# Two Strassen passes instead of two plain ones and one Strassen pass, in the second of two gated MLP blocks

## The reference, cut to what matters

```python
# block 1
n = ln(x)
s = silu(n @ w_gate.T)                     # 1376 a token
s = where(|s| is among the 688 smallest of its row, 0, s)
x = x + ln((s * (n @ w_up.T)) @ w_down.T)
# block 2
n = ln(x)
x = x + ln((silu(n @ W_gate.T) * (n @ W_up.T)) @ W_down.T)
```

## Time and profile before

| | |
|---|---|
| median of three runs | 733.29 us |
| profiled execution | 734.79 us, span 733.0 us |
| granted TensorE clock, mean | 0.998 of full speed |
| TensorE busy | 719.5 us (98%) |
| VectorE busy | 533.0 us (73%) |
| ScalarE busy | 370.0 us (50%) |
| GpSimd busy | 183.8 us (25%) |
| block 1, up to the end of down(15) | to 397.8 us of the span, chunks of block 2 among it |
| Strassen pass, products | 556.7 to 666.6 us |
| its down projections | 666.6 to 727.1 us |

### The profile page before, as it was taken

How to read it: one execution, slowest core, us unless ns; L and a number is a source line. 1 busy time by engine, 2 the same in 40 slices (tenths; PEclk the granted TensorE clock), 3 DMA queues, 4 the chain that set the end, 5 groups by cost and what they waited for, 6 DMA issues and landing times.

```text
span 733.0 us, 9630 instructions
## 1 busy us (share of the span) xinstructions
PE 719.5 (98%) x3235; PEld 603.9 (82%) x3235; DVE 533.0 (73%) x954; ACT 370.0 (50%) x592; POOL 183.8 (25%) x322
## 2 busy tenths in 40 slices
PE   8999999999999999999999999999999999999996
PEld 7888788888888888888888887888878787777885
DVE  6789688888877788897887544555557888887442
ACT  5886577767666666667645331222234333233321
POOL 0422232333322233323301000200026444520010
PEclk9999999999999999999999999999999999999999
DMA  8641435433445535565834422353414333234431
GB/s 275 195 111 60 94 107 127 119 82 118 107 129 135 124 81 140 135 160 143 295 121 117 125 42 57 58 130 72 87 32 141 116 114 108 81 125 140 146 127 43
DMA packets 109123, 86.50 MB, mean 118 GB/s; under 512 B 65520, under 2 KB 89072, under 8 KB 108880
## 3 DMA queue, kind: packets, MB, share of 16 engines
q1 hardware_dynamic: 109072, 85.88, 42.5%
HBM read 53.08 MB, written 22.09 MB: 103 GB/s over the span
## 4 chain that ended last, share of the span: by engine, by line
PE 73%; issue 8%; DVE 8%; POOL 5%; ACT 4%; DMA 1%; POOLq 0%; SPq 0%; DVEq 0%
PE gu_ps L748 16%; PE y_ps L727 12%; PE gu_ps L713 11%; PE tr_ps L713 8%; PE tr_ps L769 5%; PE gu_ps L802 5%; PE gu_ps L816 4%; PE tr_ps L802 4%; PE tr_ps L816 3%; ACT junk L940 2%; POOL move L1809 2%; PE y_ps L769 2%; POOL thr L1812 1%; PE y_ps L802 1%; DVE below L1388 1%
## 5 line engine op out<-in xcount | busy, mean ns | idle before, releaser
L940 ACT ACTIVATE junk<-absv,thr 128x1383 bf16<-128x1383 f32 x96 | 139.2, 1450 | 49.6 <-POOL thr L1812 48.9
L727 PE MATMUL y_ps<-down_hi,hT 128*128 128x512 f32 x352 | 108.9, 390 | 0.0
L727 PEld LDWEIGHTS y_ps<-down_hi,hT 128*128 128x128 f32 x352 | 66.1, 188 | 14.5
L727 PE MATMUL y_ps<-down_lo,hT 128*128 128x512 f32 x176 | 69.4, 394 | 0.8 <-DVE hT L1306 0.8
L713 PE MATMUL gu_ps<-gate_hi,xT 128*128 128x460 f32 (+1 forms) x232 | 67.2, 371 | 0.0
L713 PE MATMUL gu_ps<-up_hi,xT 128*128 128x460 f32 (+1 forms) x232 | 67.2, 371 | 0.0
L1809 POOL TENSOR_SCALAR move<-sgn 128x1 f32<-128x1 f32 x80 | 40.6, 507 | 93.2 <-ACT junk L940 93.1
L1793 POOL TENSOR_TENSOR yrstd<-yvar,half 128x1 f32<-128x1 f32 x32 | 18.7, 583 | 132.1 <-DVE yvar L1315 131.8
L1786 POOL TENSOR_TENSOR xrstd<-xvar,half 128x1 f32<-128x1 f32 x32 | 18.7, 584 | 130.2 <-DVE xvar L1278 130.2
L713 PEld LDWEIGHTS gu_ps<-up_hi,xT 128*128 128x128 f32 x232 | 43.6, 188 | 5.1
L713 PEld LDWEIGHTS gu_ps<-gate_hi,xT 128*128 128x128 f32 x232 | 43.7, 189 | 4.9
(11 more groups left out here) (329 smaller groups left out, 1813.2 us busy)
## 6 DMA issues: line engine op xcount, KB each, us to landing
absv<-prod SPq DMA_DIRECT2D x64, 176.0 KB, 3.4
xin<-x_scratch SPq DMA_DIRECT2D x20, 256.0 KB, 2.8
h_scratch<-prod SPq DMA_DIRECT2D x20, 256.0 KB, 2.5
xres<-in_L_attn_x SPq DMA_DIRECT2D x16, 256.0 KB, 5.2
x_scratch<-xres SPq DMA_DIRECT2D x16, 256.0 KB, 3.2
xin<-in_L_attn_x SPq DMA_DIRECT2D x13, 256.0 KB, 3.6
xT<-xin SPq DMA_DIRECT2D x52, 64.0 KB, 2.4
xg_even<-xin SPq DMA_DIRECT2D x48, 64.0 KB, 2.5
```

The lines of the kernel that those rows point to most:

```text
L727: last = nc.tensor.matmul(y_ps[:, :], h, w[:, c, :], start=(c == 0 and i == 0), stop=(c == JC - 1 and i == 2))
L940: nc.scalar.activation(junk[:, 0:I + PAD], absv[:, q, A0 - PAD:A0 + I], ACT.Sign, bias=thr[:, q:q + 1], scale=-1.0, accum_out=sgn[:, q:q + ...
```

## The change

The two plain groups go. Block 2 has two Strassen passes, tiles 0 to 7 and 8 to 15, 22 units in all. With it change:
- Seven products go to seven fixed banks, in the order 1, 2, 3, 6, 5, 7, 4 (`PSEQ`); product i of a unit waits until product i of the unit before has been read (`product_read`).
- The four weight sums of a chunk are the same in both passes. GpSimd makes them in block 1, in tiles 4 to 10 (`left_sum`, `SUMS_AT`), two chunks a tile and then one; SP stores them in `left_scratch`, and `load_left` loads all seven factors, in three DMAs.
- Left factors have four places a, b, c, d (`PLACES`) instead of three. `left_lo(u + 1)` stands ahead of `gate0(u)`, from unit 4 on.
- The copies of the weights in DRAM are gone. `load_down` loads the down weights once, and `split_pair_lo` for them goes from VectorE to GpSimd, in units 5 to 10 of pass 1. `right_sum` and `h1` go to GpSimd too.
- Tiles 16 to 23 (the tokens of pass 1) are normalised in block 1, two x tiles a tile in tiles 7 to 14 (`TWO`) instead of 11 to 14. Of pass 2, four x tiles are normalised in units 5 to 8 of pass 1 (`X_AT`) and four in the down tiles between the passes (`XD`).
- Units 0 to 3 of pass 1 are mixed with the end of tiles 14 and 15 of block 1.

```diff
-    PLAIN = S0 // GT
-    PSEQ7 = [1, 2, 6, 5, 3, 7, 4]
-    M_AT = {(u, i): 7 * u + n + 1 for u in range(JC) for n, i in enumerate(PSEQ7)}
+    PASSES = 2
+    S_TILES = 2 * GT
+    UNITS = PASSES * JC
+    PSEQ = [1, 2, 3, 6, 5, 7, 4]
+    M_AT = {(u, i): 7 * u + n + 1 for u in range(UNITS) for n, i in enumerate(PSEQ)}
+    PLACES = "bdcbdcabdab" + "abcabcabcab"
...
+        SUMS_AT = {4: (0, 1), 5: (2, 3), 6: (4, 5), 7: (6, 7), 8: (8,), 9: (9,), 10: (10,)}
+        PAIR_AT = {5: (0,), 6: (1,), 7: (2,), 8: (3,), 9: (4,), 10: (5,)}
+        R_AT = {2: (1,), 3: (2,), 5: (3,), 6: (6, 5), 7: (7, 4)}
+        LEFT_AT = {3: JC, 4: JC + 1}
+        X_AT = {5: 24, 6: 25, 7: 26, 8: 27}
+        XD = {0: (28,), 1: (29,), 2: (30,), 3: (31,)}
...
@@ tensor
             down(TILES - 3)
-            for m in range(2):
-                chunk(0, 0, m)
-                chunk(0, 1, m)
+            strassen(0, PSEQ[:4])
             down(TILES - 2)
-            for j in range(2, 4):
-                chunk(0, j, 0)
-                chunk(0, j, 1)
+            strassen(0, PSEQ[4:])
+            strassen(1)
+            strassen(2)
+            strassen(3)
             down(TILES - 1)
...
+            for u in range(4, JC):
+                strassen(u)
+            for r in range(S_TILES):
+                down_tile(r)
+            for u in range(JC, UNITS):
+                strassen(u)
+            for r in range(S_TILES, 2 * S_TILES):
+                down_tile(r)
...
@@ vector: hand-over from block 1, then pass 1
+            swap_h(last - 1)
+            right_lo(0, 1)
+            left_lo(0)
+            right_lo(0, 2)
+            y_stats(last - 2)
+            right_lo(0, 3)
+            right_lo(0, 6)
+            split_h_lo(last - 1)
+            add_residual(last - 2)
+            for n in range(3):
+                times_up(last, n)
...
+            for u in range(3, JC):
+                if FULL <= u < JC - 1:
+                    left_lo(u + 1)
+                gate0(u)
+                sum_u2(u)
+                if u == 4:
+                    y_stats(last)
+                sum_u4(u)
+                gate1(u)
+                if u == 3:
+                    left_lo(u + 1)
+                elif u == 4:
+                    add_residual(last)
+                elif u in X_AT:
+                    x_stats(X_AT[u])
+                    x_normalise(X_AT[u])
+                if u == JC - 1:
+                    tile_lo(0, 0)
+                sum_u3(u)
+                up1(u)
+                up0(u)
+                h0(u)
...
@@ gpsimd
-            def left_sums(u):
-                pool.wait_ge(l_in[u % 3], 32 * (u // 3 + 1))
-                a21, a22, a11, a12, s1, s2, s3, s4 = (left_raw(u, LEFT.index(i)) for i in (0, 4, 1, 2, 5, 6, 7, 3))
...
+            def split_pair_lo(k):
+                j, n = PAIRS[k]
+                pool.wait_ge(phi_done, k + 1)
+                size = P if j + n < JC else LASTJ
+                at = slice(0, size), slice(j, j + n), slice(0, H)
+                nc.gpsimd.tensor_tensor(down_lo[at], down_lo_raw[at], down_hi[at].bitcast(F32),
+                                        ALU.subtract).then_inc(plo_done, 1)
+
+            def h1(u):
+                pool.wait_ge(silu1_done, u + 1)
+                pool.wait_ge(up1_done, u + 1)
+                at = s_part("sum1", u)[0:width(u), :]
+                nc.gpsimd.tensor_tensor(at, at, s_part("gate1", u)[0:width(u), :], ALU.mult).then_inc(h1_done, 1)
...
+                for n in range(STEPS):
+                    if n == 3:
+                        if j in TWO and XSEQ[p + 2] < TILES + S_TILES:
+                            x_rstd(XSEQ[p + 2])
+                        y_rstd(j - 2)
+                    newton(j, n)
+                    for u in SUMS_AT.get(j, ())[1:] if n < 4 else ():
+                        left_sum(u, n)
             last = TILES - 1
+            right_sum(0, 5)
             units(last)
-            for n in range(3):
-                newton(last, n)
+            newton(last, 0)
+            right_sum(0, 6)
+            newton(last, 1)
+            right_sum(0, 4)
+            newton(last, 2)
+            right_sum(0, 7)
             newton(last, 3)
             y_rstd(last - 2)
             newton(last, 4)
+            h1(0)
+            for u in range(1, JC):
+                if u == 4:
+                    y_rstd(last)
+                elif u in X_AT:
+                    x_rstd(X_AT[u])
+                h1(u)
+                if u == 1:
+                    y_rstd(last - 1)
+                for k in PAIR_AT.get(u, ()):
+                    split_pair_lo(k)
```

More of the change, by code:

```diff
@@ L120, in moved, with width, earlier, sum_place @@
         return POS[a] - FIRST
-    def width(j):
-        return P if j < JC - 1 else LASTJ
+    def width(u):
+        return P if u % JC < JC - 1 else LASTJ
+    def earlier(u):
+        return PLACES.rindex(PLACES[u], 0, u) if PLACES[u] in PLACES[:u] else None
+    def sum_place(u):
+        if u < 3:
+            return (0, 2, 0)[u]
+        return u % JC % 2
+    def stores_before(u):
+        return sum(sum_place(v) == sum_place(u) and v % JC < JC - 1 for v in range(u))
     ctx = ExitStack()
@@ L1660, in _ @@
+            right_lo(0, 4)
+            left_lo(1)
+            gate0(0)
+            sum_u2(0)
             find_below(last)
-            split_h_lo(last - 1)
-            add_residual(last - 2)
-            split_pair_lo(NPAIR + 1)
+            sum_u4(0)
+            gate1(0)
             find_top(last)
+            sum_u3(0)
+            up1(0)
+            up0(0)
+            h0(0)
+            left_lo(2)
             find_flag(last)
+            gate0(1)
+            sum_u2(1)
             select(last)
+            sum_u4(1)
@@ L1667, in _ @@
+            gate1(1)
             swap_h(last)
-            times_up2(0)
-            split_h2_lo(0)
-            times_up2(1)
-            split_h2_lo(1)
+            sum_u3(1)
+            up1(1)
+            up0(1)
+            h0(1)
+            left_lo(3)
             y_stats(last - 1)
-            for k in (2, NPAIR + 2):
-                split_pair_lo(k)
+            gate0(2)
+            sum_u2(2)
+            sum_u4(2)
+            gate1(2)
             add_residual(last - 1)
+            sum_u3(2)
@@ L1736, in _ @@
+            for u in range(JC, UNITS):
+                if JC < u < UNITS - 1:
+                    left_lo(u + 1)
                 gate0(u)
```

1013 lines of the change are left out of this document (432 added, 581 removed).

## The result

The changed kernel takes 753.79 us (median of four runs, 753.49 to 753.83), the kernel before 733.60 (732.73 to 734.17): a ratio of 1.028, interval 1.026 to 1.029. I had forecast 738 with a range up to 747. The sign was right, the size was not. In what follows "the port" is, as in the prediction, the access to SBUF on which GpSimd's operations and those of VectorE that have two operands in SBUF exclude each other; "the first block" is block 1.

The account below looks back on a forecast made before the run. TensorE bounds the kernel before, VectorE pass 1 of the changed one. -20.2 us on TensorE, +24.2 in pass 1 and +1 in the first block give +5.0 on 733.29: 738 us, range 722 to 747.

Parts of the forecast that it names:

- 66 matmuls, 15.0 us: First two groups of four tiles: 42 matmuls a chunk instead of 48, 15.0 us less on TensorE.
- The loop through the left split, 5.2 us: Strassen pass: TensorE's waits for VectorE's next left split vanish when it is queued one unit ahead, 5.2 us less.
- VectorE's queue in pass 1, 10.1: Pass 1: VectorE's work sums to 145.4 us, reaching tile 0's split about 10 us after TensorE would.
- the port in it, 14.1: Pass 1: GpSimd's operations delay VectorE's, 8.8 us by weight splits and 5.3 by right sums; between 0 and 21.6.
- units 6 to 9 were to take 12 us or more: Sign expected in pass 1: unit periods of 12 us or more in units 6 to 9.
- the forecast's 505: Sign expected: pass 1's down tiles start at 505 us; nearer 491 would mean the port costs little.
- The first block, 1 us, between 0 and 7: First block: eight GpSimd sums a tile between threshold-search steps cost 1 us, between 0 and 7.
- ScalarE's 1.29 us: First block: ScalarE's wait for TensorE in the tile shown, 1.29 us, taken as slack for the added sums.
- Rival 3: First block: GpSimd's sums lengthen the threshold search, tile 15 reaches the hand-over late; +7, 745 us; chance 0.10.
- Between the passes, 0: Eight down tiles between passes: TensorE takes 60 us, VectorE has some 48 to do, so no loss.
- pass 2, 0: Pass 2: VectorE needs 8.7 of 9.5 us a unit, so TensorE sets the pace, no loss.
- my sign for being wrong there (over 9.6): Pass 2: the prediction called itself wrong if this pass is slower than 9.6 us a unit.

Follow-up runs that it names:

- e4: The kernel before, with only the next unit's left split moved to the head of a unit's queue on ScalarE and VectorE: 729.55 us.
- e5: The changed kernel, with GpSimd's down-weight splits in units 5 to 8 waiting for VectorE's left split that follows h0: 744.70 us.
- e7: The changed kernel, with each of GpSimd's six down-weight splits made by four instructions of 256 columns instead of one of 1024: 747.09 us.
- e11: The changed kernel, with the x tile's normalisation in units 5 to 8 behind up1 instead of right behind its statistics: 747.59 us.
- f2: The changed kernel with e2, e5 and e11 together, plus unit 0's first right and left splits ahead of tile 14's selection: 731.98 us.
- e1: The changed kernel, with GpSimd's 44 first-block sums cut to 2 columns a slot, loads, stores and waits kept: 740.70 us.
- e2: The changed kernel, with the same 44 first-block sums placed behind a tile's first four Newton steps, their stores later to match: 743.73 us.
- e9: The changed kernel, with each of GpSimd's eight right sums made by four instructions of 256 columns instead of one of 1024: 756.49 us.
- f3: The changed kernel, with h1 given back from GpSimd to VectorE, right behind up1: 758.05 us.

## Why the prediction was wrong, step by step

- **66 matmuls, 15.0 us.** Right: the count, and 9.52 us a unit in pass 2.
- **The loop through the left split, 5.2 us.** Right, and shown alone by e4: 4.8 us in the pass, 4.3 by the medians. Every unit from the third to the tenth takes 9.52 us there.
- **VectorE's queue in pass 1, 10.1, and the port in it, 14.1.** Together 24.2 forecast; hand-over and units 4 to 10 lost 10.5 + 12.6 = 23.1. VectorE needed 158.5 us from the split of h at 357.37 to the end of tile 0's split at 515.85, where the queue and the port had been summed to 145.4 + 14.1 = 159.5. The parts are borne out: left splits of 4.21 (3.74 for the last, narrower one), wide splits of 2.4 (2.84 with their own wait), h0 of 1.09; the four right sums stretched VectorE's operations by 2.2, 1.5, 0.5 and 1.2 us, 5.4 where 5.3 was forecast. One sign came out otherwise: units 6 to 9 were to take 12 us or more, and on TensorE unit 6 took 9.6 and unit 7 11.7. e5, e7 and e11 took single waits out, and each came off the run in full; f2 changed the order without changing the queue, and nothing came off. The down tiles begin at 515.95; the forecast's 505 counted 1 us for the first block, and 11.3 more make 516.3.
- **The first block, 1 us, between 0 and 7. This step failed: 12.3 us.** I had asked whether GpSimd had time for a sum, and took ScalarE's 1.29 us as the slack of the loop. Both questions were beside the point. The port that I charged in pass 1 instruction by instruction also lies between GpSimd's sums and VectorE's pass and three splits of h in a tile, and I did not charge it there, though the earlier trace rows show those splits at 1.76 and the earlier trace rows what a sum does to a split. Rival 3 named the mechanism and the place; its +7 was 1 us in each of seven tiles, where four sums in a row stretch VectorE by 2.1 us in a loop that had 0.5 to spare in tile 9 and none in the first two tiles (there TensorE waited 0.2 and 0.3 us for the split of h even before): 0.3 to 2.7 us a tile, 12.0 in seven. e1 shows that it is the sums, e2 that it is their place.
- **Between the passes, 0; pass 2, 0.** Off by 2.2 and 1.6. The port was left out here too. Between the passes 1.0 of the 2.2 goes when the right sums of pass 2 are made in pieces (e9); 0.5 is a start-up gap ahead of the first down tile and 0.7 a wait for the split of h in the second. In pass 2 it is mostly one wait of the first unit, whose bank is released by a residual (L1286) that comes late; the other units take 9.52. By the average of all eleven, 9.66, my sign for being wrong there (over 9.6) was just met. No run took the wait of unit 11 away.
- **The range.** By its own terms its upper end is 733.3 - 20.2 + 10.1 + 21.6 + 1 = 745.8, not 747. Nothing hangs on it: 753.8 lies outside either.

With 12.3 in place of 1 and 4.7 for all that lies behind pass 1, less 1.1 in pass 1, the forecast of 738 becomes 753.

## What to carry to other kernels

A resource that two engines lock against each other has to be charged wherever both are at work, also in stages that the change seems only to brush. Ask of each added instruction which of the other engine's instructions it will meet, and what hangs on that one. The slack of a loop is the bound's period less the loop's own length, not the wait of one engine in it. An instruction that moves to another queue brings its wait along (f3). Before giving work to a slower engine, look for a place beside operations that don't need the lock: e2, e5 and e11 moved work without removing any, and brought 22 of the 40 us back. Even so the result is not worth the change: with all three the kernel takes 731.52 us, and the kernel before with its left split moved, one small edit, 729.55.
